# Order of the work inside an attention step, rearranged on all five engines

## The reference

```python
eq, nk, nv = lin(x, n2e_q), lin(x, n2e_k), lin(x, n2e_v)
edges = ln(attn(eq, nk, nv, adj.transpose(0, 2, 1)) + x, norm1)        # pass 0
nq, ek, ev = lin(x, e2n_q), lin(edges, e2n_k), lin(edges, e2n_v)
nodes = ln(x + attn(nq, ek, ev, adj), norm2)                           # pass 1
h = gelu(lin(nodes, ffn_1), approximate=False)                         # 512 -> 2048
out = layernorm(x + ln(nodes + lin(h, ffn_2), norm3))
```

## Time and profile before

| what | value |
|---|---|
| median of 3 runs | 3084.95 us (3084.39 to 3085.16) |
| the profiled execution | 3087.05 us |
| its span, first to last instruction | 3085.3 us |
| TensorE busy | 2926.4 us, 95% of the span |
| VectorE, ScalarE, GpSimd busy | 1629.9, 1521.1, 1582.1 us |
| mean granted TensorE clock | 0.984 |

### The profile page before, as it was taken

How to read it: one execution, slowest core, us unless ns; L and a number is a source line. 1 busy time by engine, 2 the same in 40 slices (tenths; PEclk the granted TensorE clock), 3 DMA queues, 4 the chain that set the end, 5 groups by cost and what they waited for, 6 DMA issues and landing times.

```text
span 3085.3 us, 54441 instructions
## 1 busy us (share of the span) xinstructions
PE 2926.4 (95%) x17920; PEld 2416.5 (78%) x17920; DVE 1629.9 (53%) x5018; ACT 1521.1 (49%) x3882; POOL 1582.1 (51%) x1482
## 2 busy tenths in 40 slices
PE   8999999999899998999988999999999999999996
PEld 7787878777777777777777888888888888888885
DVE  6676767667766676677675223333333233333234
ACT  6666666666677777777775322222222222222221
POOL 3757566666577777777772133333332333333324
PEclk9999999999999999999999999999999999999998
DMA  6444444444556565565655211110111111101101
GB/s 196 110 108 110 114 110 117 107 109 110 128 130 166 138 164 145 152 155 143 163 133 136 76 55 55 55 47 14 54 54 48 54 54 54 49 14 53 55 35 61
DMA packets 488338, 295.64 MB, mean 96 GB/s; under 512 B 279040, under 2 KB 410240, under 8 KB 488192
## 3 DMA queue, kind: packets, MB, share of 16 engines
q1 hardware_dynamic: 488192, 294.01, 36.0%
HBM read 159.73 MB, written 67.11 MB: 74 GB/s over the span
## 4 chain that ended last, share of the span: by engine, by line
PE 48%; POOL 24%; issue 16%; ACT 6%; DVE 4%; DMA 1%; SPq 1%; POOLq 0%; DVEq 0%; ACTq 0%
PE proj L1347 23%; PE score L1361 11%; PE proj L1361 11%; POOL source_lo L663 4%; POOL att_tokens L668 3%; POOL att_v L650 3%; ACT att_probs L528 2%; POOL normed L635 2%; POOL normed L637 2%; POOL att_even_sum L635 2%; POOL att_even_sum L637 2%; POOL att_v L648 2%; PE proj L893 2%; POOL att_query_lo L657 1%; POOL att_rstd L626 1%
## 5 line engine op out<-in xcount | busy, mean ns | idle before, releaser
L1293 DVE TENSOR_TENSOR hidden_lo<-hidden,hidden_hi 128x512 fp32r<-128x512 f32 x256 | 217.0, 848 | 946.0 <-ACT hidden_hi L1130 946.0
L1137 ACT ACTIVATE hidden<-proj,ffn_bias 128x512 f32<-128x512 f32 x256 | 176.5, 689 | 1013.4 <-PE proj L1347 1013.4
L528 ACT ACTIVATE att_probs<-att_probs,att_minus_max 128x128 f32<-128x128 f32 x1024 | 398.6, 391 | 315.1 <-DVE att_minus_max L787 312.6
L663 POOL TENSOR_TENSOR source_lo<-source_raw,source_hi 128x512 fp32r<-128x512 f32 x128 | 204.8, 1621 | 295.7 <-ACT source_hi L551 295.7
L101 POOL TENSOR_TENSOR pool_scratch<-pool_scratch 128x1 f32<-128x1 f32 x144 | 30.3, 210 | 544.3 <-DVE ffn_moments L1237 485.3
L776 DVE SCALAR_TENSOR_TENSOR att_q_lo<-proj,att_bias_q,att_q_hi 128x512 fp32r<-128x512 f32 x128 | 96.1, 751 | 285.0 <-ACT att_q_hi L522 284.9
L787 DVE CUSTOM_DVE_ANT_0 att_probs<-score,att_mask 128x128 f32<-128x128 f32 x1024 | 226.4, 286 | 0.0
L893 PE MATMUL proj<-weight_v_hi,source_hi 128*128 128x512 f32 x512 | 212.6, 415 | 13.3 <-DVE weight_v_lo L746 12.4
L940 PE MATMUL score<-att_k_hi,att_q_hi 128*128 128x256 f32 x512 | 158.3, 309 | 65.9 <-DVE att_q_lo L776 65.8
L893 PE MATMUL proj<-source_hi,weight_k_hi 128*128 128x512 f32 x512 | 208.7, 408 | 5.7 <-DVE weight_k_lo L746 5.7
L796 DVE TENSOR_TENSOR att_p_lo<-att_probs,att_p_hi 128x512 f16<-128x512 f32 x256 | 204.8, 841 | 14.2 <-ACT att_p_hi L535 14.2
(11 more groups left out here) (162 smaller groups left out, 8878.7 us busy)
## 6 DMA issues: line engine op xcount, KB each, us to landing
att_tokens<-in_x SPq DMA_DIRECT2D x128, 256.0 KB, 3.0
source_raw<-in_x_t SPq DMA_DIRECT2D x16, 1024.0 KB, 6.0
edges_t<-turned SPq DMA_DIRECT2D x64, 256.0 KB, 2.5
source_raw<-edges_t SPq DMA_DIRECT2D x16, 1024.0 KB, 6.2
att_query_raw<-in_x_t SPq DMA_DIRECT2D x16, 1024.0 KB, 6.9
nodes_t<-turned SPq DMA_DIRECT2D x64, 256.0 KB, 3.1
source_raw<-nodes_t SPq DMA_DIRECT2D x16, 1024.0 KB, 7.5
normed<-nodes SPq DMA_DIRECT2D x16, 1024.0 KB, 5.6
```

The source lines that it names most:

```text
L528: nc.scalar.activation(probs[:, j, :], probs[:, j, :], ACT.Exp, bias=minus_max[:, j:j + 1], scale=-1.0, accum_out=row_sum[:, side, j:j + 1 ...
L663: nc.gpsimd.tensor_tensor(source_lo[1 - parity][:, c, :], source_raw[:, c, :], source_hi[1 - parity][:, c, :].bitcast(F32), ALU.subtract). ...
L1137: nc.scalar.activation(hidden[:, c % 2, :], up_bank[c % 2][:], ACT.Gelu, bias=bias_1[:, c:c + 1]).then_inc(activated, 1)
L1293: nc.vector.tensor_tensor(hidden_lo[:, c % 2, :], hidden[:, c % 2, :], hidden_hi[:, c % 2, :].bitcast(F32), ALU.subtract).then_inc(hidden_ ...
```

## The change

The same instructions are issued with the same operands; only their order in the engines' lists differs.

- VectorE: `value_rest` goes from the end of a step to just behind the masks of the following step; `probabilities_low` goes ahead of `key_low` and `query_low`; the low parts of weights at the two stage changes go behind `query_low`. `add_weighed` stays last.
- ScalarE: both halves of the exponentials and then both halves of `probabilities_high` go ahead of `key_high`; all four `centre` go behind `query_high`; the copies of turned tokens are moved to fit.
- TensorE: each `turn` in step 3 is moved one place forward: the first ahead of the keys, the last ahead of the scores instead of between their halves.
- GpSimd: `inverse_spread` goes ahead of `value_low` of the fourth graph, and `split_queries` ahead of the last `add_bias`.
- SP: the store of the second turned graph goes ahead of the transposes that are issued in step 3.

```diff
@@ SP
                 store_turned(sp, g - 1, before, 0)
+                store_turned(sp, g - 1, before, 1)
             turn_probabilities(sp, C * g + 2)
             if not starts(g):
-                store_turned(sp, g - 1, before, 1)
                 store_turned(sp, g - 1, before, 2)
@@ ScalarE
                 if not first:
                     exponentials(n, (u - 1) % 2, 0)
-                key_high(g, own, u)
-                if u == 2 and not starts(g):
-                    centre(act, g - 1, 1 - parity, 0)
-                if u == 3 and not starts(g):
+                    exponentials(n, (u - 1) % 2, 1)
+                turning = u == C - 1 and not starts(g)
+                if turning:
                     copy_turned(act, g - 1, 0)
-                if not first:
-                    exponentials(n, (u - 1) % 2, 1)
-                if u == 2 and not starts(g):
-                    centre(act, g - 1, 1 - parity, 1)
-                query_high(g, own, u)
-                if u == 3 and not starts(g):
-                    copy_turned(act, g - 1, 1)
                 if not first:
                     probabilities_high(n, 0)
                     probabilities_high(n, 1)
+                key_high(g, own, u)
+                if turning:
+                    copy_turned(act, g - 1, 1)
+                query_high(g, own, u)
                 if u < 2:
                     split_source(g, parity, range(2 * u, 2 * u + 2))
                 if u == 2 and not starts(g):
-                    centre(act, g - 1, 1 - parity, 2)
-                    centre(act, g - 1, 1 - parity, 3)
-                if u == 3 and not starts(g):
+                    for b in range(GB):
+                        centre(act, g - 1, 1 - parity, b)
+                if turning:
                     if own == 1 and after == 1:
                         split_queries(g + 1)
                     copy_turned(act, g - 1, 2)
+                    copy_turned(act, g - 1, 3)
...
-                if u == 3 and not starts(g):
-                    copy_turned(act, g - 1, 3)
@@ GpSimd
+            if not starts(g):
+                inverse_spread(pool, g - 1)
             value_low(g, parity, 3)
             if not starts(g):
-                inverse_spread(pool, g - 1)
...
                 gain_and_shift(pool, g - 1, 1 - parity)
-            add_bias(g, 3)
-
             if own == 1 and after == 1:
                 split_queries(g + 1)
+            add_bias(g, 3)
@@ VectorE
+                    if not first:
+                        value_rest(g, parity, 1)
+                elif u < C - 1:
+                    value_rest(g, parity, u + 1)
+                elif not at(g, last_group - 1):
+                    value_rest(g + 1, 1 - parity, 0)
+                if not first:
+                    probabilities_low(n, 0)
+                    probabilities_low(n, 1)
                 key_low(g, own, u)
+                query_low(g, own, u)
                 if u == 2 and own != after:
                     if after == 1:
                         weights_low(1, "v")
                     else:
                         feed_forward.low(dve, 0)
                         feed_forward.low(dve, 1)
-                query_low(g, own, u)
-                if not first:
-                    probabilities_low(n, 0)
-                    probabilities_low(n, 1)
                 if u < 2:
                     if not starts(g):
                         add_weighed(dve, g - 1, 1 - parity, before, u + 2)
-                    value_rest(g, parity, u + 2)
                 else:
                     add_weighed(dve, g, parity, own, u - 2)
-                    if not at(g, last_group - 1):
-                        value_rest(g + 1, 1 - parity, u - 2)
@@ TensorE
+                if turning:
+                    turn(pe, g - 1, 1 - parity, 0)
                 keys(g, parity, own, u)
                 if turning:
-                    turn(pe, g - 1, 1 - parity, 0)
+                    turn(pe, g - 1, 1 - parity, 1)
                 queries(g, parity, own, u)
...
                 if turning:
-                    turn(pe, g - 1, 1 - parity, 1)
+                    turn(pe, g - 1, 1 - parity, 2)
...
                 if turning:
-                    turn(pe, g - 1, 1 - parity, 2)
+                    turn(pe, g - 1, 1 - parity, 3)
                 scores(g, u, 0)
-                if turning:
-                    turn(pe, g - 1, 1 - parity, 3)
                 scores(g, u, 1)
```

## The result

The changed kernel takes 3053.91 us (median of four runs, 3053.77 to 3059.41) against 3085.05 for the kernel before on the same chip (3084.39 to 3085.83): ratio 0.9903, 95% interval 0.9886 to 0.992. It is faster, by 31 us where 139 were forecast, and outside the range of 2928 to 3008. The profiled execution took 3053.77, its span is 3051.9, its mean granted clock 0.986 (0.984 before).

What follows compares the result with a forecast made beforehand. TensorE was taken as the bound, losing time in attention steps: 151 us of idle and clock loss, less 12 that stays, removes 139 from 3087.05, giving 2948, or 2946 as median; range 2928 to 3008 us.

Steps and rivals of the forecast that it cites:

- The score wait in step 2: TensorE: scores wait 65.8 us in all for the queries' low part; centring behind the query split readies it at S+7.1.
- The transposes' DMA queued ahead of the keys: ScalarE: high halves wait for this DMA, keys and queries behind them; landing by S+13.0 for need at 13.9, cost nothing.
- rival 4: ScalarE: keys and queries queued behind high halves wait for the transposes; slower, 3125 us if landing takes 11 us; chance 0.05.
- rival 3: Little happens: the queries' low part stays last because of a wait not seen; 3085 us; chance 0.03.
- the earlier copies: Pass change, one group: earlier copies give back about 5 us.
- the weight split: Pass change: weight split of values moves behind query_low, so value products wait for it instead of scores, +1.5 us.
- The sum itself: Idle 109.3, hidden 11.5 and clock 30 make 151 us; 12 stay, 139 removed, giving 2946 us.
- VectorE's paragraph: VectorE: whole step fits TensorE's period; sums S+7.1 to 9.7, masks at about S-0.4, 0.8 us spare.
- rival 1: VectorE becomes the bound, low-half pairs stretched by GpSimd from 1.28 to 2.54 us; costs 39, 2985 to 3010 us; chance 0.17.
- the second transpose of step 3: TensorE asks for it 3.1 us into step 3; checked against GpSimd's gain and shift, which follow every 2.6 us.
- Rival 2: GpSimd: moments late at S+2.5, so step 2 weighing waits 0.9 us behind inverse spread and value_low(3); 2974 to 3025; chance 0.13.

Runs made afterwards that it cites:

- the last version: Changed kernel with the weighed product kept in its PSUM bank, VectorE's attention list written straight, and ScalarE's first copy ahead of the exponentials: 2946.57 us, ratio 0.955.
- the run with short sums: Changed kernel with the weighed product multiplied in place in its PSUM bank, so the sum reads one SBUF operand; orders kept: 2977.53 us, ratio 0.9653.
- the straight list: Changed kernel with the product in its PSUM bank and VectorE's attention list written without a loop, other engines still looped: 2964.98 us, ratio 0.961.

## Why the prediction was right in part and wrong in size

Right. The score wait in step 2 came from centring ahead of the query split: step 2 fell to 11.37, and one move alone does it. The transposes' DMA queued ahead of the keys cost nothing, for ScalarE's list of waits names none of them, and the high parts' landed within 6.7 us: rival 4 did not happen. Nor did rival 3. At the pass change the earlier copies gave what was told (the step went from 20.97 to 15.83, -5.1 for -5), while the weight split cost more (13.97 to 18.56, +4.6 for +1.5) and the step behind went from 13.99 to 15.28: together 0.7 lost where 3.5 were to be won.

The sum itself was right as a floor. It put idle time and clock loss at 139 us and the time without them at 2946; the last version takes 2946.6, and the same stretch of attention is 139.8 us shorter in it, with 12.1 of idle time left where 12 were told. But that version holds three moves that the prediction did not know of. What failed is the claim that nothing else is late next.

The step that failed first is VectorE's paragraph: "Sums follow, S+7.1 to 9.7 ... It just fits". A sum priced at 0.72 took 1.80 in the group read and 1.39 on the mean, so with 0.8 us of spare in a step the masks came at S+0.9 instead of S-0.4, and mending it first brings back 76 of the 107 us. This was rival 1, in its mechanism: I gave it 0.17 and 39 us, put the stretch at the low halves, and ruled it out for the sums by one row ("not stretched at 597.5 beside the same gain"). That sum began 0.18 us before the gain ended, and GpSimd's next instruction, begun inside it, took 1.60, where pieces of the same shape take 1.27 and 1.29. It was short by its place, right behind the low halves, and the change took that place away. Reading the GpSimd row beside the VectorE row would have shown that the 0.72 hung on it.

The second is ScalarE's copy. The prediction checked the second transpose of step 3 ("TensorE asks for them 3.1 ... into step 3") against the shift and not against the copy that frees its bank. By its own times the exponentials end at S+3.0 and the copy at S+3.6, so 0.5 us of wait was in its numbers: the run with short sums has 0.25 to 0.98. Late masks made it 2.0 in most groups, and behind 8 of 23 such waits the granted clock fell to 0.50, its lower level of 1.2 of 2.4 GHz. Here four transposes take 1.03 us for the 0.63 of 590.96:

```profile
343.40 1.03 PE L857 MATMUL att_turn<-att_identity,normed 128*128 128x128 f32 x4 [2.01 <-ACT turned L483]
```

The third is VectorE's loop edge, 2.4 to 3.7 us of idle time in seven places of the changed kernel, each ahead of the masks of a step 0. Mending it took 12.5 us off one version and 31.6 off another. It stood in the waits of the kernel before and was not read, since hardly anything waited for it there:

```profile
DVE att_dve_scratch L92 <- issue: 23.6, 10, 2.7
```

Rival 2 came in part: weighing waited 13.4 us in 15 places. Its cause was not GpSimd's order, as putting that back showed, but VectorE being late, as the run with short sums showed, where this wait is gone.

## What to carry to other kernels

When a reorder moves an instruction that shares a resource with another engine, its price is not the duration it has in the old trace: take the stretched one unless the trace shows which of the two will start first, and look at what stood just ahead of it and set that order. Before counting a stall as gained, list every wait that it hides, the copy that frees a buffer and the idle time without a releaser too, and work each against the new times. When a change of many parts gives less than it should, run its strongest part alone: here one move of five gave twice the whole.

## What the runs showed of the hardware

An addition of 128x512 f32 with both operands in SBUF took 0.69 to 1.87 us on VectorE in the changed kernel, longer the more of a GpSimd instruction was left when it began; with one operand left in PSUM its mean over 64 was 692 ns, whatever GpSimd did meanwhile.

VectorE stands idle 2.1 to 5.2 us before the first masks of many loop iterations with no releaser in the trace, and not at all in the straight list. A packet of an instruction queue starts at or inside each of the ten such gaps of the kernel before and the seven of the changed one. TensorE shows gaps of 2.1 to 4.4 us at its edges where an iteration holds four groups and none where it holds two; packets of the other instruction queue lie at all four, and that queue moves 121 packets instead of 53. How much of a gap is the fetch itself was not measured, and the straight list also drops the small memsets that stand at the masks in the loop.

In two runs what a wait cost beyond itself went with its length. One of 2.0 us in most groups stood with a mean clock of 0.986, two of about 0.4 and 1.0 with 0.992. Not every 2.0 us wait was followed by a lower clock, though: in the 3 us behind the one at 343.40 the granted clock was 0.50, behind the one at 590.96 it was 1.00. What tells these apart stays open.
